# Graph attention, batch by batch: K through DRAM in two exchanges of two row tiles, and its split moved ahead of x and the results

## What is computed

```
z_l, z_g, v = x @ W_lang.T, x @ W_grav.T, x @ W_V.T
A_l = relu(zn @ zn.T) * not_eye          # zn: rows of z_l over their norms
A_g = exp(-max(|z_g_i - z_g_j|^2, 0) / (2 sigma^2)) * not_eye
K_l, K_g = (A * adj) / max(row sum, eps) # for A_l and for A_g
K = w_l * K_l + (1 - w_l) * K_g          # w_l = sigmoid(gate_logit)
out = layernorm(x + (K @ v) @ W_O.T)
```

## Time and profile before

| | |
|---|---|
| median of 3 runs | 997.1 us (996.71 to 997.12) |
| the profiled execution | 998.76 us |
| its span | 997.0 us, granted TensorE clock 0.998 of full speed |
| busy: TensorE, weight loads, VectorE, ScalarE, GpSimd | 965.2, 825.5, 702.8, 323.7, 151.9 us |
| the chain that ended last | TensorE 79%, VectorE 13%, issue 3%, DMA 2%, ScalarE 2% |
| HBM traffic | 63.44 MB read, 42.47 MB written, 106 GB/s |

### The profile page before, as it was taken

One profiled execution on the slowest core, in us unless ns is written; L12 is line 12 of the kernel. 1 busy time (PEld: TensorE's weight loads), 2 busy tenths in 40 slices (PEclk: granted clock), 3 DMA queues, 4 the chain that ended last, 5 costly groups with the idle time before them and its releaser, 6 DMA issues.

```text
span 997.0 us, 13226 instructions
## 1 busy us (share of the span) xinstructions
PE 965.2 (97%) x4802; PEld 825.5 (83%) x4802; DVE 702.8 (70%) x1954; ACT 323.7 (32%) x632; POOL 151.9 (15%) x155
## 2 busy tenths in 40 slices
PE   9999999999999999999999999999999999999997
PEld 7788887888878888787888879888788888879885
DVE  4557757767776677767777677677757777676488
ACT  4333243232432424233232432424233232432331
POOL 0202111021200212111021200212002121200231
PEclk9999999999999999999999999999999999999999
DMA  8323253442534524253432524425344342623001
GB/s 221 75 48 82 95 140 102 117 142 75 133 95 112 153 82 120 96 130 123 112 127 85 143 90 111 157 79 123 96 119 135 101 124 93 148 85 127 1 22 64
DMA packets 215873, 106.78 MB, mean 107 GB/s; under 512 B 140545, under 2 KB 187649, under 8 KB 215809
## 3 DMA queue, kind: packets, MB, share of 16 engines
q1 hardware_dynamic: 213696, 104.90, 37.7%
q10 hardware_dynamic: 2112, 1.05, 0.4%
HBM read 63.44 MB, written 42.47 MB: 106 GB/s over the span
## 4 chain that ended last, share of the span: by engine, by line
PE 79%; DVE 13%; issue 3%; DMA 2%; ACT 2%; SPq 0%; POOLq 0%; POOL 0%; DVEq 0%
PE ring L326 19%; PE ring L327 18%; PE ring L328 18%; PE g_bank L326 8%; PE g_bank L328 8%; PE g_bank L327 8%; DVE whole L742 2%; DVE bn L951 2%; DVE y L944 2%; DVE xT_lo L746 2%; DMA off_turned<-off 1%; DVE kT_lo L926 1%; DMA off<-off_turned 1%; ACT kT_hi L609 1%; DVE u_odd_lo L732 1%
## 5 line engine op out<-in xcount | busy, mean ns | idle before, releaser
L732 DVE TENSOR_TENSOR zg_lo<-ring,zg_hi 128x512 fp32r<-128x512 f32 x64 | 43.9, 690 | 107.3 <-ACT zg_hi L568 107.3
L1152 POOL TENSOR_TENSOR rstd<-var_eps,neg_half 128x1 f32<-128x1 f32 x64 | 46.0, 719 | 440.4 <-DVE var_eps L959 440.4
L326 PE MATMUL ring<-xT_hi,wgT_hi 128*128 128x512 f32 x256 | 101.8, 398 | 0.1
L326 PE MATMUL ring<-xT_hi,wlT_hi 128*128 128x512 f32 x256 | 101.1, 395 | 0.0
L327 PE MATMUL ring<-xT_lo,wgT_hi 128*128 128x512 f32 x256 | 100.1, 391 | 0.0
L328 PE MATMUL ring<-xT_hi,wgT_lo 128*128 128x512 f32 x256 | 99.8, 390 | 0.0
L328 PE MATMUL ring<-xT_hi,wlT_lo 128*128 128x512 f32 x256 | 99.7, 389 | 0.0
L327 PE MATMUL ring<-xT_lo,wlT_hi 128*128 128x512 f32 x256 | 99.7, 389 | 0.0
L326 PE MATMUL ring<-wvo_hi,xT_hi 128*128 128x512 f32 x256 | 99.7, 389 | 0.0
L328 PE MATMUL ring<-wvo_hi,xT_lo 128*128 128x512 f32 x256 | 99.6, 389 | 0.0
L327 PE MATMUL ring<-wvo_lo,xT_hi 128*128 128x512 f32 x256 | 99.6, 389 | 0.0
(11 more groups left out here) (126 smaller groups left out, 2226.8 us busy)
## 6 DMA issues: line engine op xcount, KB each, us to landing
xb<-in_x_dram SPq DMA_DIRECT2D x60, 256.0 KB, 4.5
out_dram<-y SPq DMA_DIRECT2D x60, 256.0 KB, 2.0
k_turned<-ag SPq DMA_DIRECT2D x56, 256.0 KB, 2.2
al<-k_turned SPq DMA_DIRECT2D x224, 64.0 KB, 2.0
y<-in_x_dram SPq DMA_DIRECT2D x14, 1024.0 KB, 5.4
off_turned<-off SPq DMA_DIRECT2D x28, 384.0 KB, 2.3
off<-off_turned SPq DMA_DIRECT2D x112, 96.0 KB, 2.2
y<-in_x_dram SPq DMA_DIRECT2D x4, 256.0 KB, 5.5
```

What stands on the lines that cost most here:

```text
L326: nc.tensor.matmul(psum, lh, rh, start=k == 0, stop=False)
L732: nc.vector.tensor_tensor(pair[1][:, i, :], bank[:, :], pair[0][:, i, :].bitcast(F32), ALU.subtract).then_inc(evacuated, 1)
L1152: nc.gpsimd.tensor_tensor(rstd[:, i:i + 1], var_eps[:, i:i + 1], neg_half[:, 0:1], ALU.pow)\
```

## The change

Three parts. SP stores K's row tiles in pairs, 512 KB each, both pairs ahead of any fetch; a pair is fetched in four DMAs of 128 KB, and a semaphore counts a pair. ScalarE writes kT_hi of row tiles 1 to 3 ahead of all four parts of xT_hi. VectorE makes the first two x transposes ahead of row tile 0's kT_lo, splits row tiles 1 to 3 right behind the last u, and has the x splits and the results behind them, with the other two x transposes among them.

```
-        k_by_part = k_turned.rearrange("t (b j) (d r) -> t d j b r", j=Q, d=QN)
-        k_stored = [sem(f"k_stored{i}") for i in range(T)]
-        k_loaded = [sem(f"k_loaded{i}") for i in range(T)]
+        k_by_part = k_turned.rearrange("t (b j) (d r) -> d j (t b) r", j=Q, d=QN)
+        k_stored = [sem(f"k_stored{h}") for h in range(T // 2)]
+        k_loaded = [sem(f"k_loaded{h}") for h in range(T // 2)]
...
             def turn_k(b):
-                for i in range(T):
-                    sp.wait_ge(k_blocks, b * T + (i + 1))
-                    sp.dma_start(k_turned[i], ag[:, i, :]).then_inc(k_stored[i], 16)
-                    if i:
-                        fetch_k(b, i - 1)
-                fetch_k(b, T - 1)
-
-            def fetch_k(b, i):
-                sp.wait_ge(k_stored[i], b * 16 + 16)
-                for d in range(QN):
-                    sp.dma_start(al[d * Q:(d + 1) * Q, i, :].rearrange("j (b r) -> j b r", b=QN),
-                                 k_by_part[i, d]).then_inc(k_loaded[i], 16)
+                for h in range(T // 2):
+                    pair = slice(2 * h, 2 * h + 2)
+                    sp.wait_ge(k_blocks, b * T + (2 * h + 2))
+                    sp.dma_start(k_turned[pair].rearrange("t p n -> p t n"), ag[:, pair, :]).then_inc(k_stored[h], 16)
+                for h in range(T // 2):
+                    pair = slice(2 * h, 2 * h + 2)
+                    sp.wait_ge(k_stored[h], b * 16 + 16)
+                    for d in range(QN):
+                        sp.dma_start(al[d * Q:(d + 1) * Q, pair, :].rearrange("j t (b r) -> j (t b) r", b=QN),
+                                     k_by_part[d, :, 2 * h * QN:(2 * h + 2) * QN, :]).then_inc(k_loaded[h], 16)
...
                 def hi_k(self, i):
-                    act.wait_ge(k_loaded[i], self.b * (16 * QN) + 16 * QN)
+                    act.wait_ge(k_loaded[i // 2], self.b * (16 * QN) + 16 * QN)
...
                 s.hi_k(0)
                 s.hi("u", 1, 3, u[1 - parity])
-                s.hi_k(1)
+                for i in range(1, T):
+                    s.hi_k(i)
                 for k in range(T):
                     whole_hi_part(b + 2, k, xT)
-                    if k + 2 < T:
-                        s.hi_k(k + 2)
...
                 s.lo("u", 1, 0, u_next)
                 s.lo("u", 1, 1, u_next)
+                x_transpose(b + 2, 0)
+                x_transpose(b + 2, 1)
                 s.lo_k(0)
                 s.lo("u", 1, 2, u_next)
-                s.lo_k(1)
-                x_transpose(b + 2, 0)
                 s.lo("u", 1, 3, u_next)
-                for i in range(T):
-                    if i + 1 < T:
-                        x_transpose(b + 2, i + 1)
-                    whole_lo_part(b + 2, i, xT)
-                    s.residual(0, i)
-                    s.row_sums(0, i)
-                    if i + 2 < T:
-                        s.lo_k(i + 2)
-                    s.statistics(0, i)
-                    if i:
-                        s.normalise(0, i - 1)
+                for i in range(1, T):
+                    s.lo_k(i)
+                whole_lo_part(b + 2, 0, xT)
+                s.residual(0, 0)
+                x_transpose(b + 2, 2)
+                s.row_sums(0, 0)
...
                 s.normalise(0, T - 1)
```

More of the change, by code:

```diff
@@ L1006, in batch @@
                 s.lo("u", 1, 1, u_next)
+                x_transpose(b + 2, 0)
+                x_transpose(b + 2, 1)
                 s.lo_k(0)
                 s.lo("u", 1, 2, u_next)
-                s.lo_k(1)
-                x_transpose(b + 2, 0)
                 s.lo("u", 1, 3, u_next)
-                for i in range(T):
-                    if i + 1 < T:
-                        x_transpose(b + 2, i + 1)
-                    whole_lo_part(b + 2, i, xT)
-                    s.residual(0, i)
-                    s.row_sums(0, i)
-                    if i + 2 < T:
-                        s.lo_k(i + 2)
-                    s.statistics(0, i)
-                    if i:
-                        s.normalise(0, i - 1)
+                for i in range(1, T):
[4 more added lines that the diff above has]
+                s.row_sums(0, 0)
+                whole_lo_part(b + 2, 1, xT)
+                s.statistics(0, 0)
+                x_transpose(b + 2, 3)
+                s.residual(0, 1)
+                s.normalise(0, 0)
+                s.row_sums(0, 1)
+                whole_lo_part(b + 2, 2, xT)
+                s.statistics(0, 1)
+                whole_lo_part(b + 2, 3, xT)
+                s.residual(0, 2)
+                s.normalise(0, 1)
+                s.row_sums(0, 2)
+                s.statistics(0, 2)
+                s.residual(0, 3)
+                s.normalise(0, 2)
+                s.row_sums(0, 3)
+                s.statistics(0, 3)
                 s.normalise(0, T - 1)
```

## The result

| | before | after |
|---|---|---|
| median of 6 runs each | 996.9 us (996.04 to 1000.79) | 991.92 us (990.06 to 993.17) |
| ratio, 95% interval | | 0.9943 [0.9924, 0.9962] |
| profiled execution, span | 998.76, 997.0 us | 992.3, 990.6 us |
| granted TensorE clock | 0.998 | 0.997 |

The change makes the kernel faster by 5.0 us, 0.6%. 976.9 was predicted, with a range of 970 to 988: the direction was right, the size was a quarter of the forecast.

The account below looks back on a forecast made before the run. TensorE, busy 97% of the span, was taken as the bound, with gains only from its gaps: 25.8 - 3.5 - 2.1 = 20.2 us off 998.76 gives 978.6, or 976.9 us on the median's scale; range 970 to 988.

Parts of the forecast that it names:

- The order's 25.8 us: VectorE's new order: K splits in time, TensorE's waits ahead of third and fourth products go, 14 x 1.84 = 25.8 us.
- VectorE's cover: VectorE's x splits and results behind K: 0 extra cost, ending near 241.5, with half a microsecond to spare.
- The store: SP's 512 KB store of a K pair: lands in 2.7 us, with 2.3 to 4.4 kept as range.
- The issues: SP's fetches of the first pair: begin at 219.95, 0.47 us per issue, the fourth issued at 221.36.
- the rival in which issues grow with their pieces: SP's fetch issues take 1.31 us like the x loads: 15 us slower, 1012; chance 0.04.
- the term for the traffic behind the second store: DMA engines: second store's 512 KB delay the first pair's fetch by at most 0.55 us; half taken, landed at 224.0.
- the charge of 0.25 us a batch: TensorE's small gap ahead of the first product, from tile 0 landing at 224.0: 3.5 us in all.
- ring order: DMA engines take descriptors in ring order: whole 0.55 us falls on pair 0, 0.45 a batch, time 980.
- The one stray transfer, 2.1 us: K's exchange: tile 0's slack is spent, so a stray slow transfer costs its whole length; one charged, 2.1 us.
- The exchange lands later: Rival: the 512 KB store takes 3.3 us, time 985; at 4.4, 1.95 a batch, 4 us above before; chance 0.18.
- VectorE's tail: Rival: results behind K run over 0.6 us longer, delaying the next Gram exchange: 984; chance 0.05.
- The signs: Right: K-split waits under 5 us, ahead of first products. Wrong: store over 3.3, issue over 0.7, line 832 waits in most batches.

Follow-up runs that it names:

- e1: The changed kernel with the exchange of before (four stores of 256 KB, each fetched by four DMAs of 64 KB), new order on ScalarE and VectorE kept: 975.13 us.
- e6: e1 with ScalarE's order of before, so the single-tile exchange and only VectorE's order new: 972.82 us.
- e5: The changed kernel with the second pair's store issued by ScalarE, behind its first copy of u, on another DMA queue: 1003.06 us.
- e3: The changed kernel with SP fetching each pair ahead of the other pair's store (store, fetch, store, fetch): 992.36 us.
- e4: The changed kernel with SP fetching the second pair only when the first has landed: 990.67 us.

## Why the prediction was wrong

**The order's 25.8 us: right as a wait.** By e1 and e6 the new order takes out all of the 25.7 us. The splits of tiles 1 to 3 are in time in every batch. The time itself fell by 22.1 us in e1 and by 25.0 in e6.

**VectorE's cover: nearly right.** "The work that is now behind K" costs nothing in after: the Gram wait is 2.2 us, 2.9 before. But there the late first product gives VectorE more time. In e1 and e6, without that, the Gram wait is 4.6 and 4.0, so 1 to 2 us come back.

**The store: nearly right.** 2.7 us were taken for 512 KB. The shortest is 2.8, and 2.8 is the median of e5's first stores, as of those in after. The median of all 28 in after, 3.1, holds the second ones, which took 3.1. The Trainium skill ("DMA: Bandwidth & Descriptors", Anatomy of one DMA) has a fit for the GpSimd path that gives 3.2 us for this size, as an estimate; the measured 2.8 lies under it, as 2.2 did at 256 KB.

**The issues: right but for one.** The first fetch was forecast 5.54 us ahead of an undisturbed first product (219.95 against 225.49); in the seventh batch it is 463.48 - 457.86 = 5.62. The median issue is 0.45 us against 0.47, so the rival in which issues grow with their pieces fell. But the second fetch of the first pair takes 0.86 us behind the store, so the fourth is issued 1.97 us behind the first instead of 1.41. With no store ahead in the same queue the second takes 0.45 in e3 and 0.47 in e5's ninth batch. The slow issue isn't the cause by itself: e5 hasn't got it, and its tile 0 comes later still.

**The step that failed** is the term for the traffic behind the second store: "At most some 0.55 us of delay come of it. I take half: landed at 224.0", and with it the charge of 0.25 us a batch, 3.5 in all. Landing at 224.0 is 1.49 us ahead of an undisturbed product; in the seventh batch kT_hi begins at 462.99, 0.49 ahead of it. That is 1.0 us later than charged, in nine batches like this, and more in five. Three things were too small. The half was taken without a reason, and cost 0.3. The store's traffic was put at 1.33 us, so that the fetches would flow 1.7 us behind their first issue; they flow 2.0 behind it (459.87), and 0.95 with nothing ahead (e3). And the fetches were sized on "185 GB/s at a share of 0.62 is 298 at full share, so 512 KB are 1.76 us": at that rate fetches that have been held back catch up with SP, which needs 1.88 us to issue four. They don't. With the engines full they move 250 GB/s (the windows above), so 524,288 bytes take 2.1 us, longer than SP takes to issue them. All the time for which the store keeps them out is lost. In e3, with nothing ahead, the same fetch lands 4.0 us behind its first issue (457.45 to 461.45); in after it takes 5.1 (457.86 to 462.99). Of these 1.1 us the fetches' later start is 1.06 (2.01 less 0.95), and the second pair's fetch at most the 0.1 of e4. The rest of the path was right: from kT_hi to the product the prediction had 1.48 us (224.0 to 225.48), and the seventh batch has 1.51 (462.99 to 464.50). By this the charge at 224.3 should have been 0.3 more than at 224.0, so 0.55 and not 0.45.

The Trainium skill ("DMA: Bandwidth & Descriptors", HWDGE ordering), whose ring order gave 0.45 a batch in the prediction, agrees with the windows in what goes first; its charge was too small by the same rates.

**The one stray transfer, 2.1 us.** Nine batches lose 1.1 to 1.35 us each, 10.7 in all. The other five lose 1.67, 2.02, 1.71, 2.10 and 1.92, which is 3.5 us over nine's mean of 1.19. That tile 0's slack is spent was right: in the eleventh batch of e1 one issue of its fetch took 1.70 us, and no product waited. But I counted one stray where there are five. One had a store of 4.9 us and one an issue of 1.39; for the others the fetches landed in 3.6 to 3.9. Why single transfers are longer stays open.

The sum with what was measured: 25.7 - 14 x 1.19 - 3.5 = 5.5 us instead of 20.2. From 998.76 that gives 993.2; the profiled execution took 992.3.

**The rivals.** "The exchange lands later" named the right event and the wrong transfer: it let the store's landing grow, which it hardly did, and 11.8 us of gain remain by it where there were 5.6. Its upper end, 1.95 a batch, lies beyond the 1.19 measured; the range held only its nearer half. VectorE's tail was not the bound in after. In e3 the results did end late and the Gram rows waited, as described, though the reason was new: VectorE stood waiting for the second pair.

**The signs.** TensorE's wait on K stands ahead of the first product and kT_hi of tile 0 begins with a landing, both as foretold; the 16.5 us were to be under 5, and the four products with the gap ahead of them took 12.0 us in the seventh batch where 10.9 to 11.3 were named. Of the three signs that I gave for "wrong", a wait on line 832 came only twice, and a store over 3.3 us twice in 28. The third, an issue over 0.7, came in 13 of 14 batches, at the second fetch of the first pair in twelve of them; the median of all issues hides it. For the fetch's own landing, which was the term that failed, I had named no sign.

## What to carry to other kernels

Before you merge transfers, ask how many bytes must have moved, counting those queued ahead, until the first consumer can start: merging saved issues on an engine that wasn't the bound, and doubled both numbers for the tile that is needed first. A rate scaled up from a window in which the DMA engines weren't full is a hope; take it from a window in which they were full with the same pieces, or bound it. And try each part of a change alone: here one engine's new order was worth 2.5%, and the rest of the change took three quarters of it back.

## What the runs showed of the hardware

The clock. After some of TensorE's longer waits its granted clock is half, 1.2 GHz, and the matmuls behind the wait lose again. Windows of e5 around its longest K wait, 3.12 us up to 828.55 (the third number from the end is the granted clock, 1.00 for 2.4 GHz):

```profile
825.50:826.00 0.50, 0.00 (x0) 0.00 (x0) 0.00 (x0) 0.00 (x0) 0.00 (x0) 1.00 0.87 166
...
828.00:828.50 0.50, 0.00 (x0) 0.00 (x0) 0.50 (x2) 0.50 (x2) 0.00 (x0) 0.50 0.06 15
...
829.00:834.00 5.00, 5.00 (x13) 3.84 (x13) 3.01 (x6) 2.16 (x4) 0.00 (x0) 0.50 0.00 0
...
835.00:836.00 1.00, 1.00 (x6) 0.82 (x5) 1.00 (x3) 0.54 (x1) 0.00 (x0) 1.00 0.00 0
```

TensorE is idle, the clock falls late in the wait, stays at 0.50 while the first product's matmuls start 0.43 us apart, and is back before 835. This batch lost 6.24 us, of which 3.28 are the gap itself. In e4 the clock fell 1.1 us behind the end of a wait of 1.87 us, and in e3 late in one of 2.90 (0.50 from 312 to 314). It did not fall after the longest wait of after, 1.86 us up to 822.38:

```profile
820.00:822.00 2.00, 0.53 (x3) 0.10 (x1) 0.46 (x1) 1.12 (x3) 0.00 (x0) 1.00 0.86 164
...
823.00:825.00 2.00, 2.00 (x11) 1.64 (x10) 2.00 (x4) 1.96 (x4) 0.00 (x0) 1.00 0.00 0
```

Nor did it after 2.50 us in e1. So the wait's length alone doesn't tell which it will be, and a late transfer can cost nearly twice its delay.
